# Rounding the head sums of an RWKV block into two one-pass products, with new orders on four engines

## What is computed

```python
def step(s, rkvw):
    r_t, k_t, v_t, w_t = rkvw
    a = k_t[..., :, None] * v_t[..., None, :]
    out = jnp.einsum('bhi,bhij->bhj', r_t, u * a + s)
    s = a + w_t[..., :, None] * s
    return (s, out)
...
og = out.reshape(b, l, h, s_)                      # 32 heads of 16 channels
m = og.mean(-1, keepdims=True)
va = ((og - m) ** 2).mean(-1, keepdims=True)
og = ((og - m) / jnp.sqrt(va + 1e-05)).reshape(b, l, e) * gn_w + gn_b
x1 = x + og * g @ Wo.T
xc = _ln(x1, ln2_w, ln2_b)
...
return x1 + rr * (kk @ Wfv.T)
```

## Time and profile before

| what | value |
|---|---|
| times of three runs | 1409.76, 1414.32, 1417.7 us; median 1414.32 |
| profiled execution, its own time | 1411.06 us |
| its span in the profile | 1409.2 us |
| start of `maa_second` in step 3 and in step 15 | 746.33 and 1297.56 us |
| time from there to the end of the span | 111.6 us |

### The profile page before, as it was taken

How to read it: one execution, slowest core, us unless ns; L and a number is a source line. 1 busy time by engine, 2 the same in 40 slices (tenths; PEclk the granted TensorE clock), 3 DMA queues, 4 the chain that set the end, 5 groups by cost and what they waited for, 6 DMA issues and landing times.

```text
span 1409.2 us, 42786 instructions
## 1 busy us (share of the span) xinstructions
PE 1329.8 (94%) x17120; PEld 936.5 (66%) x17120; DVE 929.5 (66%) x2431; ACT 734.7 (52%) x1772; POOL 492.5 (35%) x550
## 2 busy tenths in 40 slices
PE   4899999999999999987899999999999999999977
PEld 4677777777777777655666667666676667666634
DVE  3455555555555555456578878787888787887863
ACT  4676766766777666542334443545344534543332
POOL 2322222222222211113455345634554355534540
PEclk9999999999999999989899999999999999999979
DMA  5433322222222222213000010001000101010000
GB/s 169 138 94 106 100 69 69 71 75 75 75 75 75 75 69 65 89 43 135 21 21 10 26 28 21 13 24 27 21 14 22 27 22 27 9 27 21 15 14 13
DMA packets 47145, 73.70 MB, mean 52 GB/s; under 512 B 21413, under 2 KB 24101, under 8 KB 45445
## 3 DMA queue, kind: packets, MB, share of 16 engines
q1 hardware_dynamic: 46981, 71.24, 16.8%
HBM read 60.24 MB, written 7.57 MB: 48 GB/s over the span
## 4 chain that ended last, share of the span: by engine, by line
PE 80%; DVE 8%; issue 6%; DMA 3%; SPq 1%; ACT 1%; POOL 1%; DVEq 0%; ACTq 0%; POOLq 0%
PE b_bank L1824 18%; PE b_bank L1830 12%; PE ring_bank L696 6%; PE ring_bank L697 5%; PE ring_bank L698 5%; PE av_bank L782 4%; PE b_bank L1938 4%; PE score_banks L755 4%; DVE probs L443 3%; PE b_bank L1975 3%; PE score_banks L742 2%; PE b_bank L1964 2%; PE b_bank L1878 2%; DVE probsT L460 2%; PE av_bank L768 2%
## 5 line engine op out<-in xcount | busy, mean ns | idle before, releaser
L1119 POOL TENSOR_TENSOR rst<-rp,st 128x448 f32<-128x448 f32 x192 | 210.1, 1117 | 59.6 <-DVE st L1342 57.7
L443 DVE CUSTOM_DVE_ANT_0 probs<-score_banks,unmask 112x375 f32<-112x375 f32 x256 | 124.8, 545 | 93.0 <-issue 93.0
L588 ACT ACTIVATE probs<-probs,least_inv 112x375 f32<-112x375 f32 x256 | 152.4, 606 | 32.6 <-DVE least_inv L443 32.6
L460 DVE SCALAR_TENSOR_TENSOR probsT<-score_banks,least_cols 125x448 f32<-125x448 f32 x192 | 108.0, 618 | 54.4 <-PE score_banks L755 51.7
L603 ACT ACTIVATE probsT<-probsT,key_mask 125x448 f32<-125x448 f32 x192 | 114.6, 661 | 47.9 <-DVE probsT L460 47.7
L1111 POOL TENSOR_TENSOR xm<-mixed,xa 128x448 f32<-128x448 f32 x80 | 88.5, 1107 | 143.6 <-DVE mixed L1271 137.3
L337 POOL TENSOR_TENSOR aT_lo<-whole,aT_hi 128x375 fp32r<-128x375 f32 x64 | 58.9, 920 | 194.7 <-ACT whole L569 192.6
L696 PE MATMUL ring_bank<-aT_hi,wk_lo 128*128 128x376 f32 x256 | 91.2, 356 | 2.4 <-issue 2.4
L371 POOL TENSOR_TENSOR ctx_rstd<-ctx_var_eps,a_eps_exp 125x3 f32<-125x3 f32 x16 | 13.8, 864 | 214.6 <-DVE ctx_var_eps L416 214.6
L697 PE MATMUL ring_bank<-aT_lo,wk_hi 128*128 128x376 f32 x256 | 85.5, 334 | 0.0
L698 PE MATMUL ring_bank<-aT_hi,wk_hi 128*128 128x376 f32 x256 | 85.4, 334 | 0.0
(11 more groups left out here) (183 smaller groups left out, 3108.5 us busy)
## 6 DMA issues: line engine op xcount, KB each, us to landing
least_cols<-values_of_two_batches SPq DMA_DIRECT2D x32, 437.5 KB
ctx_tok<-in_ctx SPq DMA_DIRECT2D x16, 750.0 KB
xT_sb<-in_xT SPq DMA_DIRECT2D x16, 224.0 KB, 3.0
inv_cols<-values_of_two_batches SPq DMA_DIRECT2D x128, 28.0 KB, 4.1
x_tok<-in_x SPq DMA_DIRECT2D x16, 224.0 KB, 2.6
x_between_layers<-x_tok SPq DMA_DIRECT2D x16, 224.0 KB, 4.5
b_x<-x_between_layers SPq DMA_DIRECT2D x16, 224.0 KB, 3.0
x_post<-x_between_layers SPq DMA_DIRECT2D x16, 224.0 KB, 2.8
```

What stands on the lines that cost most here:

```text
L443: dve.tensor_tensor_reduce(out=probs[:, g % 2, i], in0=score_bank[0:T, i, 0:TC], in1=unmask[:, m[1]], scale=-SCALE, scalar=-LOWEST, op0=AL ...
L460: dve.scalar_tensor_tensor(out=probsT[:, g % 2, k].rearrange("p (i t) -> p i t", t=T), in0=score_bank[0:TK, :, k * T:(k + 1) * T], scalar= ...
L588: act.activation(probs[:, g % 2, i], probs[:, g % 2, i], ACT.Exp, scale=-1.0, bias=least_at(m, g, i), accum_out=sums[:, g, i:i + 1]).then_ ...
L1119: pool.tensor_tensor(by_chunk(rst[:, j % NPROD]), by_chunk(rp[:].rearrange("p c t -> p (c t)")), state_of(j), ALU.mult).then_inc(s_pprod, 1)
```

## The change

1. **Two rounded passes.** `same_head` is copied to a float32r tile `heads_r`. For each group r of near products ACT writes a rounded copy `rg_hi` (`near_high`) and DVE subtracts it from `rg`, which leaves the rest in `rg_lo` (`near_low`, printed by its tile `rg_r`). `attend_near` multiplies `heads_r` with both halves into one bank. The same is done for the group norm: ACT rounds `wkv` (`norm_high`), POOL writes the rest (`norm_low`), PE multiplies both by `centring`, which is one minus the head's mean, so the centred value comes out of PE and DVE's `centre` goes. ACT squares it twice, once whole and once rounded (`square`, `square_high`), POOL subtracts (`square_low`), and PE multiplies both halves with `mean_r`.
2. **Groups.** The near products are grouped (1), (2, 7), (3, 6), (4, 5), 392 columns each, where they had been 448, 448, 448 and 224.
3. **Orders.** The queues of all four engines are written anew for steps 3 to 15; the early steps get an order of their own, close to the old one.
4. Some tiles share memory (`fin` with `ln2_tok`, `x2` with `x1_post`), so the load of `x1_post` waits for `out_ready` of the batch before, and `apply2` waits for the store of the batch before. Two pairs of constants share a semaphore.

```diff
-GROUPS = [(1, 7), (2, 6), (3, 5), (4,)]
+GROUPS = [(1,), (2, 7), (3, 6), (4, 5)]
...
+        def norm_low(l):
+            pool.wait_ge(s_gnhi, count(l, 2, 1))
...
+            low, high = norm_parts(l)
+            pool.tensor_tensor(low, wkv[:], high.bitcast(F32), ALU.subtract).then_inc(s_gnlo, 1)
+
+        def square_low(l):
+            pool.wait_ge(s_sq, count(l, 1, 1))
+            pool.wait_ge(s_gnhi, count(l, 2, 2))
+            pool.tensor_tensor(norm_parts(l)[1], norm_home(l)[1], wkv_r[:].bitcast(F32), ALU.subtract).then_inc(s_gnlo, 1)
...
+        def near_low(m, r):
+            dve.wait_ge(s_rghi, count(m, QUAD, r + 1))
+            dve.tensor_tensor(group(rg_lo, r), group(rg, r), rg_hi[:, r % 2].bitcast(F32), ALU.subtract).then_inc(s_rglo, 1)
...
-        def centre(l):
-            dve.wait_ge(s_mean, count(l, 1, 1))
...
+        def near_high(m, r):
+            act.wait_ge(s_rg, count(m, QUAD, r + 1))
+            if r >= 2 or at_least(m, 1):
+                act.wait_ge(s_arep, count(m, QUAD, r - 1))
+            act.copy(rg_hi[:, r % 2], group(rg, r)).then_inc(s_rghi, 1)
...
+        def norm_high(l):
+            act.wait_ge(s_wkv, count(l, 1, 1))
...
+            act.copy(norm_parts(l)[1], wkv[:]).then_inc(s_gnhi, 1)
...
+        def square_high(l):
+            act.wait_ge(s_cen, count(l, 1, 1))
+            act.activation(wkv_r[:].rearrange("p c t -> p (c t)"), norm_bank(l)[0][:, 0:CT], ACT.Square).then_inc(s_gnhi, 1)
...
-            pe.matmul(near_bank[r % 2][:, 0:z - a], same_head[:], rg[:, a:z], start=True, stop=True).then_inc(s_arep, 1)
+            dst = near_bank[r % 2][:, 0:RG_END[0]]
+            pe.matmul(dst, heads_r[:], rg_hi[:, r % 2], start=True, stop=False)
+            pe.matmul(dst, heads_r[:], group(rg_lo, r), start=False, stop=True).then_inc(s_arep, 1)
...
+            pe.matmul(norm_bank(l)[0][:, 0:CT], centring[:], high, start=True, stop=False)
+            pe.matmul(norm_bank(l)[0][:, 0:CT], centring[:], low, start=False, stop=True).then_inc(s_cen, 1)
```

More of the change, by code:

```diff
@@ L1149, in last_steps @@
             rec_key(m)
+            norm_low(l)
+            square_low(l)
             product(m, 0)
@@ L1163, in last_steps, with early_step @@
             rstd2(l)
+            norm_low(m)
+            square_low(m)
             gate_output(m, False)
             rstd2(m)
[L1167 to L1171, removed]
+        def early_step(n, pre, scan, post):
             p, m, l, more = later(n, 1), later(n, -1), later(n, -2), pre and not is_batch(n, B - 1)
-            early = is_batch(n, 1) or is_batch(n, 2)
-            if more and not early:
-                rstd1(p)
             if scan:
@@ L1211, in step @@
                 xa_state(p)
+        def step(n, pre, scan, post):
+            if is_batch(n, B):
+                return last_steps()
+            if is_batch(n, B + 1):
+                return
+            if is_batch(n, 1) or is_batch(n, 2):
+                return early_step(n, pre, scan, post)
+            p, m, l, more = later(n, 1), later(n, -1), later(n, -2), pre and not is_batch(n, B - 1)
+            if scan:
+                rec_key(m)
+            if post:
+                norm_low(l)
+            if pre:
+                mix(n, 0)
+            if post:
+                square_low(l)
+            if pre:
+                mix(n, 1)
+            if scan:
+                product(m, 0)
+                product(m, 1)
+                product(m, 2)
+            if post:
+                gate_output(l, scan)
+            if pre:
+                mix(n, 2)
+            if scan:
+                product(m, 4)
+                product(m, 5)
+            if pre:
+                mix(n, 3)
+            if scan:
+                product(m, 6)
+            if post:
+                rstd2(l)
+            if pre:
+                mix(n, 4)
+            if scan:
+                product(m, 8)
+                product(m, 9)
+            if more:
+                rstd1(p)
+                xa_state(p)
+            if scan:
+                product(m, 10)
+                product(m, 12)
+                product(m, 13)
+                product(m, 14)
         def rest():
```

389 lines of the change are left out of this document (299 added, 90 removed).

## The result

The changed kernel takes 1453.2 us (1451.6 to 1459.68, four runs) beside 1412.04 us for the kernel before: a ratio of 1.0293 with a 95% interval of 1.0264 to 1.0323. It is slower by 2.9%, where I forecast 1405 us and gave 1388 to 1426 as the range. Its profiled execution spans 1449.8 us, 40.6 more than before. The starts of the steps (`maa_second`, x32) divide that into three: step 3 begins at 751.03 instead of 746.33 (+4.7), the twelve steps 3 to 14 take 582.30 instead of 551.23 us (+31.1), step 15 and the drain (the steps after it, in which the last two batches are finished) 116.5 instead of 111.6 (+4.8).

A forecast was written before the change was run, and what follows sets the result against it. PE's own work was taken to bound steady steps: 14.0 + 30.6 + 0.3 = 44.9 us against 45.95, -13.6 over 13 steps. With +4.5 for early steps and drain, total -9 gave 1405 us, range 1388 to 1426.

The forecast's parts named there:

- PE's work per step: Steady steps: rounded attend groups and group norm products cut PE's work by 1.91 us a step, bounds 1.5 and 2.2.
- The order in front of `wo`: From `maa_second` to `wo`: 14.0 us instead of 14.96, with waits of about 0.5 at the variance and for ACT's value.
- The wait at `transpose_x`: Behind `wo`, PE waits for DVE's `apply1`: 0.3 us a step taken, bounds 0 to 2.2.
- side case: Values arrive late for `chunk_sums`, each step waiting 0.7 us, or the clock makes waits cost twice; 1414 us, chance 0.05.
- The chain's length: DVE's operations from `residual` to the end of `apply1`, ahead of `transpose_x`: 11.0 to 12.2 us.
- The early steps: Steps 1 and 2: `scan` starts later behind `near_low`, at about 662.1 in step 1; +3.5 and +1, together +4.5 us.
- The drain: Last batches: a longer group norm chain, about +0.7 us each at the variance, beside PE's other work; cost 0.
- the slower rival: DVE becomes the bound at `transpose_x`; at 2.2 us of wait a step takes 46.8, the kernel 1430 us; chance 0.17.
- three signs of being wrong: Wait at L2050 over 1 us, `near_low` mean above 0.9 us, or PE waiting for a DMA ahead of `chunk_sums`.

The follow-up runs named there:

- e6: Changed kernel with DVE's subtraction for the fourth near group moved ahead of the residual sum; 1408.27 us, ratio 0.9982 to the kernel before.
- e2: Kernel before, float32 products and centring on DVE kept, with only the new queue orders of steps 3 to 15; 1410.22 us, ratio 0.9997.
- e5: Changed kernel with six of POOL's products of each batch cut to one column, their sums missing from the result; 1401.86 us, ratio 0.9916.
- e7: Changed kernel with POOL waiting for `apply1` before its last three products of a step; 1418.93 us, ratio 1.0062.
- e10: e2 plus one unread DVE difference of 280 columns in the place of the fourth subtraction; 1468.6 us, ratio 1.0363.
- e1: Changed kernel with `apply1` moved on DVE ahead of the third product and `shift2`; 1457.8 us, ratio 1.0346.
- e3: Changed kernel's rounded arithmetic in the old queue orders of steps 3 to 15; 1481.92 us, ratio 1.0501.
- e8: Changed kernel with the edits of e6 and e7 together; 1407.71 us, ratio 0.9976.
- e11: e6 with the near products attended in float32, so only the group norm is rounded; 1397.56 us, ratio 0.9877.
- e4: Changed kernel with two unread float32 matmuls of 512 columns added on PE ahead of `transpose_x`; 1434.9 us, ratio 1.0166.

## Why the prediction was wrong

- **PE's work per step** was nearly right. PE is busy 45.49 us in step 9 before and 43.17 us in a step of e6, 2.3 less, where I had 1.91. Of this 0.5 is the orders' alone (44.98 in e2), which the sum left out. An attend group took 0.50 us from start to start in the sum, 0.53 in the trace (999.26 to 999.79). With the wait gone (e6) the twelve steady steps take 532.72 us, 44.4 each against 45.9: 1.5 us saved, where my sum has 1.05.
- **The order in front of `wo`** was right to 0.1 us, with its two waits, if a little smaller: 0.33 for `square_low`, 0.26 for the value.
- **The wait at `transpose_x`** is the step that failed, where I wrote "I take 0.3, because POOL has to wait for the second `reduce` just when DVE does `shift2`". The range beside it, 0 to 2.2, held nearly: the mean of the twelve is 27.0 / 12 = 2.25 us (1.98 to 2.78). The reason I gave is true and points the other way. POOL does wait for the second `reduce` (2.58 us), and that lines its three products up with the two DVE operations that PE needs next. e5, e7 and e10 show it: held back in e7, these three give 1.36 us of the chain back. The rest of the excess is made by the additions of the near values beside POOL's mix and earlier products, which e5 ends but for one. PE's room was also 12.1 us and not 12.4, since `residual` begins 3.82 us after `wo` and not 3.63.
- **The clock** I put into a side case only ("waits of that size cost twice") and not into the wait at `transpose_x`. By the rows of step 8 the wait costs 1.7 us more than the 0.3 assumed, and the slow stretch behind it 1.6: the transposes take 0.80 us to the next row instead of 0.38 (e6), the receptance product 4.67 instead of 3.44. Together 3.3 us a step; 48.5 measured on average less 44.9 predicted is 3.6. For the rival I put the step at 2.2 us of wait at 46.8 us, 1430 in all; with its clock that is 48.4. The clock's share is less sure than the wait's: the receptance product is slow in all twelve steps of the changed kernel, but in ten of twelve in e10, with a wait of 2.8 us in each, and in eight of twelve in e1, with 2.4. What decides it beside the wait is open.
- **The chain's length** I summed at 11.0 to 12.2 us. It is 11.2 with most POOL products out (e5), 11.8 in e2, 11.7 in e6, 14.0 in the changed kernel and 15.0 in e10. The sum was good and the collisions were the error. I allowed "up to three such operations could cost 0.78 each". The trace has five: 0.60 on the 336 columns (1.11 against 0.51), 0.35 on the 56 (0.62 against 0.27), 1.15 on the 280 (1.60 against 0.45), 0.71 on the receptance input and 0.64 on `apply1`, 3.45 us in all; without them the chain would be 10.6. The Trainium skill (SBUF — State Buffer, "Who interferes with whom") calls the ports that the two engines share an exclusive lock; 1.15 us, as long as a whole POOL product, agree with it. My bound from the longest product of the earlier trace rows was too low for one operation. I had put the price of a whole POOL instruction on the four `near_low` alone; the one in this chain took 0.56 us, and the collisions fell on its neighbours.
- **The early steps**: +4.5 predicted, +4.7 measured, and the scan of step 1 began at 660.92 where I had 662.1. By e2 and e10 the start of step 3 scatters by as much, so that agreement is no proof. Seven other kernels with the changed kernel's early steps (e1, e3 to e8) reach step 3 at 753.65 to 759.76, 7 to 13 us behind the kernel before, so the 4.7 looks like luck: by those runs the early steps cost more.
- **The drain** I put at 0. Step 15 and the drain take 4.8 us more in the changed kernel. PE waits there 2.55 us for `norm_low` of the last batch, and 0.40, 2.29 and 1.59 for `square_low`; before, the waits for the group norm in that stretch were 0.75 and 0.58. These waits do not explain the 4.8 us: e11 has them too (2.55, 0.40, 1.68 and 1.59), and its stretch is 112.2 us. Some 1.2 us are the clock, in the two feed-forward key products (4.64 and 4.95 us against 5.11 and 3.29 before). The rest is open; e2, with the drain of before, has 114.0.
- **The chances**: the slower rival had 0.17 and was the right one, with its place and its releaser. It should have had more, since I knew that the room was 0.2 to 1.4 us and that POOL overlapped the chain.
- **The signs**: of the three signs of being wrong that I set, two came. The wait at L2050 is over 1 us, and `near_low` has a mean of 0.91 us (L1395, 908 ns, x64) where I counted 0.57: its median is 566 ns and its longest 1432. The third, a wait for a DMA ahead of `chunk_sums`, stands once in the trace, 1.4 us in step 1, and in the kernel before as well.

## What to carry to other kernels

Where two engines must meet within a few tenths of a microsecond, don't sum durations alone: lay the third engine's rows beside the chain and ask what starts it. If the same event starts it as sends PE towards the meeting, a chain that isn't done by then collides in every step. Keep an instruction that isn't on such a chain out of it, even one of half a microsecond, when there is an idle piece ahead. And take from a change the part that earns: here the group norm's rounding with the new orders and groups, without the near products' rounding, is 1.2% faster than the kernel before. No run has the new groups and orders without any rounding, so what the group norm's rounding earns by itself isn't shown.

## What the runs showed of the hardware

- One DVE instruction acted with many times its own length: an instruction of 0.44 us, which put the next back by 0.36, made the chain 3.2 us longer and the average step 5.0 (50.5 against 45.5).
- A row of DVE beside a POOL product holds its waiting time in its duration. `apply1` (512 columns, one SBUF tensor and per-partition scalars) took 1184 ns in the median of the changed kernel and 540 in e1, with no idle time shown ahead of it. Four operations of the receptance input took 3.21 us in e1 and 1.07 in e6. POOL can be the one that waits: the same three products took 2.92 us in e10, where DVE was held, and 3.85 in e2, where DVE's rows kept their usual length.
- After a wait of 1.98 us PE ran 5.5 us at a mean granted clock of 0.70, and after one of 2.80 us (e10) its eight matmuls of 512 columns took 5.30 us instead of 3.60. The wait alone doesn't decide it: in steps 4 and 6 of e10 the clock stayed at 1.00 after 2.80 us, and at the end of the program a wait of 3.31 us was followed by 64 matmuls in 3.29 us in e11 and before, in 4.95 in the changed kernel and in 6.17 in e6. After 0.62 us (e7), and after 1.06 us with two matmuls put ahead of it (e4), it stayed at 1.00. In the slow stretch of the changed kernel the weight loads of the receptance product start 0.85 us apart at first and 0.43 later: the two levels, 1.2 and 2.4 GHz.
